# Graph attention layer: the load of W moved from SyncE's queue to ScalarE's, behind a's rows

## What is computed

```
h   = relu(layernorm(x))                 # 4096 x 256
hw  = h @ W.T
src = hw @ a1 ; dst = hw @ a2
e   = leaky_relu(src[:, None] + dst[None, :], 0.2)
e   = where(adj == 0, -9e15, e)
out = x + softmax(e, axis=1) @ hw
```

## Time and profile before

| | us |
|---|---|
| median of 3 runs | 384.68 |
| lowest and highest | 384.57, 385.04 |
| the profiled execution, its own time | 385.12 |
| its span, first to last instruction | 383.1 |
| PE busy | 374.8 (98%) |
| DVE busy | 364.0 (95%) |
| ACT busy | 194.2 (51%) |
| POOL busy | 43.0 (11%) |

### The profile page before, as it was taken

The page is one execution under the profiler, slowest core; times in us unless marked ns, Lnnn a source line. Parts: engine busy times, 40 slices in busy tenths (PEclk is TensorE's granted clock), DMA queues, the critical chain, the costliest instruction groups (busy, mean ns, idle before and its releaser), DMA issues.

```text
span 383.1 us, 9235 instructions
## 1 busy us (share of the span) xinstructions
PE 374.8 (98%) x3368; PEld 331.4 (87%) x3368; DVE 364.0 (95%) x457; ACT 194.2 (51%) x270; POOL 43.0 (11%) x67
## 2 busy tenths in 40 slices
PE   6999899999999999999999999999999999999996
PEld 5898688888888888888888888888888888888885
DVE  4999999999999999999999999999987999999965
ACT  4899945554434644344445544444446443444330
POOL 3789002000000001110000002100000011100000
PEclk9999999999999999999999999999999999999999
DMA  7910376767576666776666667766655567766503
GB/s 239 371 78 2 127 236 219 236 211 250 186 231 223 204 216 213 251 225 227 213 222 207 214 215 229 236 223 218 218 206 189 165 216 244 231 218 224 167 2 110
DMA packets 25840, 77.69 MB, mean 203 GB/s; under 512 B 2900, under 2 KB 8280, under 8 KB 25816
## 3 DMA queue, kind: packets, MB, share of 16 engines
q1 hardware_dynamic: 24528, 74.20, 59.0%
q0 software_dynamic: 1280, 3.16, 2.2%
q10 hardware_dynamic: 8, 0.00, 0.0%
HBM read 73.14 MB, written 4.21 MB: 202 GB/s over the span
## 4 chain that ended last, share of the span: by engine, by line
PE 94%; DVE 2%; DMA 1%; POOL 1%; issue 0%; ACT 0%; SPq 0%; DVEq 0%
PE ps L1402 88%; PE ps L1209 2%; PE ps L1224 2%; PE ps L1230 2%; PE ps L1235 2%; DMA x_sb<-x 1%; POOL hn_sb L395 1%; DVE rows_sb L1113 0%; DVE p_sb L761 0%; DVE stats L720 0%; DVE d_top L931 0%; ACT p_hi L500 0%; DVE inv_den L1109 0%; DVE den L1107 0%; SPq L327 0%
## 5 line engine op out<-in xcount | busy, mean ns | idle before, releaser
L1402 PE MATMUL ps<-v_sb,p_hi 128*128 (+2 forms) x2048 | 251.3, 273 | 1.0 <-ACT p_hi L500 1.0
L510 ACT ACTIVATE p_hi<-p_sb,gp 128x1024 f16<-128x1024 f32 x126 | 144.5, 1150 | 166.7 <-DVE p_sb L780 139.1
L1402 PEld LDWEIGHTS ps<-v_sb,p_hi 128*128 128x128 f16 x2048 | 200.0, 98 | 25.9 <-issue 1.3
L787 DVE SCALAR_TENSOR_TENSOR p_lo<-p_sb,gp,p_hi 128x1024 f16<-128x1024 f32 x126 | 161.2, 1282 | 7.2 <-ACT p_hi L510 6.7
L780 DVE SCALAR_TENSOR_TENSOR p_sb<-c_row,gp,adj_sb 128x1024 f32<-128x1024 uint32 (+1 forms) x126 | 161.0, 1283 | 0.0
L1402 PE MATMUL ps<-v_sb,p_lo 128*128 (+1 forms) x1024 | 142.6, 273 | 0.0
L1402 PEld LDWEIGHTS ps<-v_sb,p_lo 128*128 128x128 f16 x1024 | 100.2, 98 | 12.4
L447 POOL DMA_DIRECT2D out<-rows_sb x24 | 13.0, 544 | 258.2 <-DVE rows_sb L1080 258.1
L395 POOL TENSOR_SCALAR hn_sb<-x_sb,moments,rstd 128x256 f32<-128x256 f32 x16 | 20.4, 1282 | 9.6 <-DVE rstd L729 9.1
L1209 PE MATMUL ps<-ident_a,hn_sb 128*128 128x128 f32 x64 | 12.1, 276 | 2.2 <-POOL hn_sb L395 2.2
L739 DVE SCALAR_TENSOR_TENSOR hnt_lo<-ps,hnt_hi 128x256 f16<-128x256 f32 x32 | 12.8, 407 | 0.1
(11 more groups left out here) (87 smaller groups left out, 89.5 us busy)
## 6 DMA issues: line engine op xcount, KB each, us to landing
adj_sb<-adj_t SPq DMA_DIRECT2D x128, 512.0 KB, 4.7
x_sb<-x SPq DMA_DIRECT2D x7, 512.0 KB, 9.0
out<-rows_sb POOLq DMA_DIRECT2D x24, 128.0 KB, 4.6
c_row<-c_flat SPq DMA_DIRECT2D x3, 512.0 KB, 5.8
out<-rows_sb SPq DMA_DIRECT2D x8, 128.0 KB, 1.7
x_sb<-x SPq DMA_DIRECT2D x2, 256.0 KB, 4.1
w_nat<-w SPq DMA_DIRECT2D x1, 256.0 KB, 2.8
c_flat<-c_blocks POOLq DMA_DIRECT2D x4, 4.0 KB, 2.9
```

The source lines that it names most:

```text
L510: nc.scalar.activation(p_hi[:, u % R, :], p_sb[:, u % R, :], ACT.Copy, scale=p_scale[:, bass.ds(t, 1)])\
L787: nc.vector.scalar_tensor_tensor(out=p_lo[:, u % R, :], in0=p_sb[:, u % R, :], scalar=p_scale[:, bass.ds(t, 1)], in1=p_hi[:, u % R, :], op ...
L1402: return nc.tensor.matmul(ps[:, k, 0:width], part[:, u % R, k * P:(k + 1) * P], v_sb[:, bass.ds(t, 1), v, 0:width], start=start, stop=stop ...
```

## The change

The instruction that issues the load of W goes from the front of SP's stream to ACT's stream, behind the two issues of a1 and a2. Its size, its target and its semaphore stay. SP's stream now begins with chunk 0 of x.

```diff
         @block.sync
         def _(sp):
-            sp.dma_start(w_nat[:], w_v).then_inc(w_nat_loaded, 16)
             for m, (t0, t1) in enumerate(X_CHUNKS):
                 sp.dma_start(x_sb[:, t0:t1, :], x_v[:, t0:t1, :]).then_inc(x_loaded[m], 16)
...
             for n, a in enumerate((a1, a2)):
                 act.dma_start(a_rows[n * KC:(n + 1) * KC, :], a.rearrange("(c p) -> c p", p=P)).then_inc(a_loaded, 16)
+            act.dma_start(w_nat[:], w_v).then_inc(w_nat_loaded, 16)
+
             def split_hn_hi(t):
```

## The result

The changed kernel takes 386.18 us in the median of 14 runs (385.19 to 387.59), the kernel before 384.99 in the same comparison (384.57 to 385.53). The ratio is 1.0027, with a 95% interval of 1.0015 to 1.0038. I had forecast 384.8 and a range up to 385.8. Not only the median moved: the times of the changed kernel lie 2.4 us apart, those of before 1.0.

A forecast was written before the change was run, and what follows sets the result against it. The head before about 11 us was taken to bound the kernel, dense PE work following. 384.68 plus 0.0 for SP, 0.0 for the table load and +0.1 for W gave 384.8 us, range 384.1 to 385.8.

The forecast's parts named there:

- What bounds, and that the shift is passed on one to one: PE is dense from about 11 us, so what the head gains or loses before then moves the end equally.
- SyncE's part, 0.0: SP's issues move 0.50 us ahead, but full DMA engines keep chunk 2 at 8.1: gain 0.0.
- The cover of the table load: On ACT, W's issue delays the table load to about 2.3; 1.32 us of idle time covers it: cost 0.0.
- The landing of W: W, issued on ACT's queue at about 1.8, was taken to land at 5.5; +0.1 us in the sum.
- The byte count: W and chunk 1 share the DMA engines from about 3 us, 524 KB at 284 GB/s: W landed by 5.65.
- my high end: Latest landing of W, with chunk 1 beside it: 6.73, when the last of the first 768 KB landed.
- The rule on queues: DMA engines go round between queues with work, so W gets about half of them and finishes about together with chunk 1.
- The price of a late W: Through std_of(0) on ACT, the chain moves by (landing - 5.5): 0 at 5.5, +0.4 at 5.9, +1.2 at 6.73.
- 1.2 us of slack: On DVE, the norm at 6.29 waits behind tiles 2 and 3's statistics until 7.50, so w_scale tolerates 1.2 us.
- The clock: Rival, 0.07: PE idles some 0.5 us for W, its clock rises later; low until 13 us costs +1.0.
- The likeliest case: The whole kernel takes 384.5 to 385.1 us, around the forecast 384.8; chance 0.60.
- the late W: Rival, 0.20: on ACT, std_of(0) waits for W; landing at 5.9 to 6.73 costs 0.4 to 1.2 us.

The follow-up runs named there:

- w_act_first: The changed kernel with W issued first on ScalarE's queue, ahead of a's rows, and chunk 0 first on SyncE's: 386.08 us, ratio 1.0032 to the kernel before.
- w_third_sp: The kernel before with W still on SyncE's queue but issued third, behind chunks 0 and 1: 386.13 us, ratio 1.0034.
- std_first: The changed kernel with the first square root, std_of(0), ahead of the wait for W on ScalarE: 386.72 us, ratio 1.0044 to the kernel before.
- after_orders: The changed kernel with waits for W moved behind work not needing W on ScalarE, DVE and PE: 386.48 us, ratio 1.0042 to the kernel before.
- after_again: The changed kernel, unedited, measured and traced once more: 386.92 us, ratio 1.0047 to the kernel before.
- w_second_sp: The kernel before with W on SyncE's queue issued second, behind chunk 0 and ahead of chunk 1: 384.87 us, ratio 0.9995.
- before_idle: The kernel before with PE also waiting for the second aggregate ahead of W's first block: 385.26 us, ratio 1.0012.
- w_alone: The changed kernel with SyncE waiting for W's landing before it issues chunk 2: 386.10 us, ratio 1.0041 to the kernel before.
- after_halves: The changed kernel with chunks 0 and 1 of one tile each, so 256 KB stand ahead of W: 385.04 us, ratio 0.9995 to the kernel before.
- fill: The changed kernel with three more keep_busy matmul pairs on PE ahead of its wait for W: 386.45 us, ratio 1.0041 to the kernel before.

## Why the prediction was wrong, point by point

**What bounds, and that the shift is passed on one to one: right.** Span less first L1231 is constant to 0.1 us in nearly all traces.

**SyncE's part, 0.0: right in what mattered.** Chunk 0 landed at 3.8 (forecast 3.72), chunk 2 at 8.15 (forecast 8.1). Chunk 1 came much earlier than I had it, at 4.4, because W hardly shared the engines with it. I had said that nothing would come of it, and so it was, though partly because the late W hid it.

**The cover of the table load: right.** L515 moved by 0.49 and L517 not at all.

**The landing of W: the step that failed.** I took 5.5 and 6.73 for the latest, and so put W into the sum at +0.1 us; it was worth 1.2 in the median. The landing was 6.01, 7.53, 7.05, 6.77, 8.09 and 6.72 in the six traces in which W stood behind 512 KB on ScalarE's queue. The byte count supposed that W and chunk 1 take turns from 3 us on. The rows of the two queues show that W's first packets go out between 3.4 and 3.9, some 1.6 to 2.1 us behind its issue, when chunk 1 is nearly done, and that its last ones are then caught beside the 512 KB of chunk 2. And my high end was no bound: it was one landing of one execution (chunk 1, third in line, at 6.73), and a load has landed only with its last packets. A sample of one says little about how late these can be. Why they are so late stays open.

**The rule on queues.** The Trainium skill (DMA: Bandwidth & Descriptors, Queues, rings and completion order) says that an engine goes round between queues that have work. That agrees with the stretch from 4.4 to 4.9, in which both move (87 and 44 packets), and with w_act_first (193 and 150). In the half microsecond ahead q10 moved 131 packets and q1, with chunk 2 issued at 1.93, only 16: up to there the service followed the issues. Whether q1 had work for the engines by then no row shows, so this doesn't decide about the rule; what failed was to reckon from the rule as if a load had work for the engines from its issue on. The Trainium skill's other rule (DMA: Bandwidth & Descriptors, Issuing engines are not separate DMA queues) is that issuing from several engines only saves issue time. That agrees with w_third_sp beside the changed kernel: W landed 4.24 and 4.23 us behind its issue.

**The price of a late W: the formula fits, its reason is incomplete.** I wrote (landing - 5.5). By it the spans should be 383.1 plus 0.5, 2.0, 1.6, 1.3, 2.6 and 1.2; measured were 0.5, 2.3, 1.5, 1.3, 2.2 and 1.1. But I had put the price on std_of(0) alone and given w_scale 1.2 us of slack. std_first showed w_scale to be as late as std_of(0) (1.95 us idle), and after_orders that W's own chain of 5.3 to 5.9 us was as late as both. The slack of 1.2 us was read between the norm and DVE's arrival in the trace of before; with std_of(0) out of the way DVE arrives 1.2 us sooner and the slack is gone. Even by my own numbers it wasn't 1.2 at a landing of 5.5: the norm moves with each landing after 4.8, so it would be there at 6.29 + 0.7 = 7.0, 0.5 ahead of DVE. In the changed kernel's trace the two meet, the statistics over at 7.80 and the norm at 7.81. And since the clock was low on most of this way in all six traces, the fit is for that clock alone.

**The clock.** It did come up later, near 10 us and in after_again only about 13.5. That PE's idle time is the reason isn't shown (w_second_sp). With W in time its price is small: 0.1 us in the trace of before_idle, a ratio of 1.0012 (0.9997 to 1.0027), none in w_second_sp. I had priced 1.0 us, but that needed a low clock to last into the dense part, which it did in after_again. How much of that trace's 2.3 us is the clock can't be parted from W's 7.53; by the formula it is 0.3, and the formula fits traces in which the clock was low too.

**The chances.** The likeliest case was given 0.60, the late W 0.20. The late W is what happened in both traces, and 12 of the 14 executions lie above the longest of before's, 385.53. Of my figures for the landing (5.2, 5.65, 6.6) I went by those of chunk 0 and of the bytes; the nearest single row was chunk 1's 4.8 us from a start within 0.15 us of W's, which gives a landing of 6.6, and by the formula 384.99 + 1.1 = 386.1, the measured time.

## What to carry to other kernels

A load that is moved to another engine's queue doesn't leave the line: count the bytes that are issued ahead of it, and take its landing from the row of the transfer that had that place before, not from its own row. Then follow the moved data's own chain to the first point where it meets the rest; the distance there (5.3 to 5.9 us here, of 7.4) says how much lateness is free. Reordering the waits bought nothing in the two orders tried here (std_first, after_orders). A load has landed only with its last packets, so give it a range of some microseconds where the engines are full: six landings of the same load lay 2.1 us apart.

## What the runs showed of the hardware

- The first 256 KB issued on SyncE's queue landed at 3.6 to 3.9 us (at 4.4 in w_act_first, with W issued beside it), the second at 4.4 to 4.8, the third, on either queue, at 5.3 to 8.1. With nothing behind it (w_alone) the third came 0.8 us behind the second, which is what its bytes need at the 333 GB/s of the earlier trace rows, an estimate; with chunk 2 behind it 1.6 to 3.5 us in the six traces of the late W. after_halves is a case between, where W came at 5.8 with 256 KB ahead of it. Why a few packets of the third place are so late stays open.
- Small loads suffer too: a's 1 KB behind W on ScalarE's queue took 3.44 us to land and moved their reader from 4.05 to 5.63.
- The clock of PE rose near 5 us in the kernel before and near 10 in w_second_sp, where PE had hardly any idle time in between (4.74 of 4.80 us busy). It can also fall again: in fill it was high at 7.4 and low at 10.6 (the pair of L1174 took 0.39 and then 0.64 us), after PE had been idle 1.42 us ahead of 7.09. What decides about its rise isn't shown.
